# VectorE takes a tile's residual behind both softmax sums and the reciprocals, not between the sums

## What is computed

```python
x = x + cross_attention(layernorm(x), ctx)       # 16 heads of 32, 77 keys a batch
x = x + moe(layernorm(x))

# cross_attention: softmax(clip(q @ k.T * scale)) @ v, then @ Wo + bo
# moe: 8 experts, the 2 best logits of each token, softmax over the two,
#      at most 1024 tokens an expert (by rank), relu(tokens @ W1.T) @ W2.T,
#      times the gate, added back at the tokens' rows
```

## Time and profile before

| | us |
|---|---|
| median of 3 runs | 1440.36 |
| lowest, highest | 1437.39, 1440.61 |
| the profiled execution | 1436.3 |
| its span, first to last instruction | 1434.5 |

### The profile page before, as it was taken

One profiled execution on the slowest core, in us unless ns is written; L12 is line 12 of the kernel. 1 busy time (PEld: TensorE's weight loads), 2 busy tenths in 40 slices (PEclk: granted clock), 3 DMA queues, 4 the chain that ended last, 5 costly groups with the idle time before them and its releaser, 6 DMA issues.

```text
span 1434.5 us, 30528 instructions
## 1 busy us (share of the span) xinstructions
PE 1310.6 (91%) x12267; PEld 778.2 (54%) x12330; DVE 954.4 (67%) x1808; ACT 805.5 (56%) x1272; POOL 732.4 (51%) x781
## 2 busy tenths in 40 slices
PE   7649999989998999996849999999999999999996
PEld 3436777767676777674536444444444444444442
DVE  8668898889889887888775545454554545455421
ACT  4557888878998899987354515133341513334210
POOL 3187888877887778787323242242414123241301
PEclk9869999999999999998969999999999999999998
DMA  6147899978897786789433564655546455654401
GB/s 197 52 95 186 209 228 227 233 187 199 208 228 164 192 192 169 181 213 223 112 131 98 162 181 137 154 176 147 149 125 188 137 155 163 158 140 126 102 17 42
DMA packets 319574, 228.88 MB, mean 160 GB/s; under 512 B 253305, under 2 KB 253689, under 8 KB 319434
## 3 DMA queue, kind: packets, MB, share of 16 engines
q1 hardware_dynamic: 304074, 176.28, 50.0%
q0 software_dynamic: 15360, 50.66, 12.0%
HBM read 118.98 MB, written 50.86 MB: 118 GB/s over the span
## 4 chain that ended last, share of the span: by engine, by line
PE 74%; DVE 10%; POOL 7%; issue 4%; ACT 2%; SPq 2%; DMA 1%; DVEq 0%; POOLq 0%; ACTq 0%
PE ps L1208 23%; PE ps L1194 23%; PE ps L1094 9%; PE ps L1024 7%; PE ps L1075 3%; PE ps L1111 2%; PE ps L1008 2%; POOL sd L544 2%; DVE sm L1459 1%; PE ps L1047 1%; DVE x L1481 1%; PE ps L997 1%; POOL qT L524 1%; POOL ph L550 1%; POOL oT L530 1%
## 5 line engine op out<-in xcount | busy, mean ns | idle before, releaser
L1194 PE MATMUL ps<-xT,w1s 128*128 128x512 f16 (+1 forms) x1632 | 336.4, 368 | 1.9 <-DVE xT L1724 1.5
L1208 PE MATMUL ps<-w2s,hT 128*128 128x512 f16 x1536 | 332.8, 379 | 0.0
L846 ACT ACTIVATE hT<-ps 128x512 f16<-128x512 f32 (+1 forms) x136 | 77.8, 572 | 356.2 <-PE ps L1194 356.2
L1194 PEld LDWEIGHTS ps<-xT,w1s 128*128 128x128 f16 x1632 | 160.7, 99 | 175.4 <-issue 1.9
L1208 PEld LDWEIGHTS ps<-w2s,hT 128*128 128x128 f16 x1536 | 150.2, 98 | 181.3
L595 POOL DMA_INDIRECT out_dram<-ys,idx x64 | 71.7, 1120 | 278.4 <-DVE ys L1764 278.4
L1024 PE MATMUL ps<-xnT,wqh 128*128 128x256 f16 x1536 | 198.5, 282 | 3.8 <-ACT partq L734 3.7
L1094 PE MATMUL ps<-woh,oT 128*128 128x512 f16 x768 | 178.9, 381 | 9.4 <-POOL oT L530 3.6
L1754 DVE SCALAR_TENSOR_TENSOR hT<-ps,hT 128x512 f16<-128x512 f32 (+1 forms) x136 | 88.6, 658 | 138.4 <-ACT hT L846 138.3
L1764 DVE SCALAR_TENSOR_TENSOR ys<-ps,gs,og 128x512 f32<-128x512 f32 x64 | 48.0, 751 | 189.8 <-PE ps L1208 189.8
L550 POOL TENSOR_TENSOR ph<-sd,ph 128x1232 f16<-128x1232 f32 x64 | 162.3, 2535 | 18.8 <-ACT ph L757 18.1
(11 more groups left out here) (206 smaller groups left out, 1982.4 us busy)
## 6 DMA issues: line engine op xcount, KB each, us to landing
xr<-x SPq DMA_DIRECT2D x64, 256.0 KB, 3.5
xrow_dram<-x SPq DMA_DIRECT2D x64, 256.0 KB, 3.7
out_dram<-x SPq DMA_DIRECT2D x64, 256.0 KB, 4.0
stage<-w1T SPq DMA_DIRECT2D x8, 2048.0 KB, 9.5
stage<-w2T SPq DMA_DIRECT2D x8, 2048.0 KB, 8.4
xt<-x SPq DMA_DIRECT2D x59, 256.0 KB, 3.3
xs<-x SPq DMA_DIRECT2D x56, 256.0 KB, 4.2
wqf<-wq SPq DMA_DIRECT2D x1, 1024.0 KB, 7.3
```

The source lines that it names most:

```text
L1194: ins = pe.matmul(hb[z][:, 0:wide], w1s[e % 2][:, a, k, ic * P:(ic + 1) * P], xT[:, 4 * b + k, cols], start=(k == 0 and i == 0), stop=(k = ...
L1208: ins = pe.matmul(yb[z][:, :], hT[:, a, k, s * P:(s + 1) * P], w2s[e % 2][:, b, k, :], start=(k == 0 and i == 0), stop=(k == 7 and i == 2))
```

## The change

In the loop over beats -7 to 54 on VectorE, `residual(h)` moves from between the two sums to behind the reciprocals, and `add_slots` from ahead of the second sum to behind it. Nothing is added or removed, and no other engine's list changes. The loop over beats 55 to 63 has this order of sums, reciprocals and residual before and after.

```diff
@@ -1818,16 +1818,16 @@
                     route = ranking((h - 22) // 16)
                     steps(route, 1)
                 s_sum(h + 5, 0)
-                residual(h)
+                s_sum(h + 5, 1)
                 if H:
                     add_slots(H)
-                s_sum(h + 5, 1)
                 for g in ones_at(h):
                     value(g)
                 if H:
                     next_batch(H[-1])
                 steps(route, 4)
                 s_recip(h + 5)
+                residual(h)
                 tx_lo(h + 11)
                 ln2_stats(h)
                 ln2_aggr(h)
```

## The result

| | before | after |
|---|---|---|
| median of 6 runs, us | 1440.48 | 1455.05 |
| lowest, highest | 1437.39, 1445.77 | 1453.79, 1457.35 |
| the profiled execution (span) | 1436.3 (1434.5) | 1456.4 (1454.6) |
| ratio of times, 95% interval | | 1.010 (1.0086 to 1.0114) |

The changed kernel is 14.6 us slower. The forecast was 1464 with a range of 1446 to 1474: the direction and the mechanism held, the size was 9 us too large.

A forecast was written before the change was run, and what follows sets the result against it. TensorE was taken to set the pace, with hardly any idle time. Terms 0.8 - 3.6 + 5.6 + 4.4 + 3.1 + 3.6 + 13.2 = 27.1 us, 24 reaching the tail, made 1460.3, carried to the median 1464 (range 1446 to 1474).

The forecast's parts named there:

- the mechanism: Beats 0 to 54: value and steps ahead of the residual, some queueing behind GpSimd's L550, delay it and stall TensorE's L1075.
- L1075 waits for the residual: Sign to look for on TensorE: such waits in some 30 beats, together 35 to 45 us, in place of hardly any.
- the waits for L530: Sign to look for: TensorE's waits for GpSimd's low half of the attention output in beats 4 and 12 should be gone.
- odd beats without steps: Sign to look for: from one projection to the next, odd beats without routing keep their length.
- The sum: Beats 0 to 54: all gains and losses make TensorE 27.1 us late at beat 55; 24 us reach the tail.
- GpSimd's gain: Beats 4, 12, 28 and 44: the earlier reciprocal starts GpSimd sooner and removes TensorE's waits for L530, -3.6 us in all.
- Beats 2 and 10: Beats where VectorE itself is late: they lose 0.4 us each, +0.8.
- Value alone: Seven even beats without routing, 24 to 46: value queues behind L550 ahead of the residual, 0.6 to 0.9 us each, +5.6.
- The steps: Beats 16 to 23, 32 to 40, 48 to 54: routing steps delay the residual, +4.4, +3.1, +3.6, and +13.2 with value.
- L785: Beat 20: the first step of choice needs this ScalarE instruction, so L1075 starts at 318.27, not 316.80, 1.5 us lost.
- The tail: From beat 55: TensorE waits 4.58 us there for work following GpSimd, which is only some 24 us late; 24 us reach it.
- Rival (d): Waits over 2 us in beats 34, 50 and the tail lower the granted clock: up to 1474; chance 0.78 together with forecast.

The follow-up runs named there:

- e6: Changed kernel in its own order, with value reading its row of 64 numbers from PSUM in place of SBUF: 1446.63 us, ratio 1.0050.
- e7: e6 with ScalarE's exponential L785 moved ahead of two other ScalarE instructions in beats 20, 36 and 52: 1446.75 us, ratio 1.0053.
- e9: Changed kernel reordered so only the routing steps stand between both sums and the residual; slots, value and reciprocals follow it: 1456.21 us, ratio 1.0061.
- e4: Changed kernel with the residual right behind both sums, then slot addition, value, steps, and reciprocals last; first run 1433.48 us against 1439.07, ratio 0.9961.
- second run of e4's order: The kernel e4 again, unchanged, on another chip where the kernel before took 1448.80 us: 1448.13 us, ratio 1.0000.
- e1: Changed kernel with slot addition, value and next_batch moved behind the residual, steps and reciprocals staying ahead of it: 1453.08 us, ratio 1.0093.
- e10: Kernel before with only the routing steps moved, behind the reciprocals and L1425: 1457.08 us, ratio 1.0133.
- e8: Changed kernel with steps and reciprocals moved behind the residual, so only value and slots stand between sums and residual: 1455.02 us, ratio 1.0055.
- e4's third run: The kernel e4 a third time, unchanged, on a third chip: 1451.60 us against 1455.21 for the kernel before, ratio 0.9975.

## Why the prediction was right, and where its size was off

**What bounds it, and the mechanism: right.** TensorE sets the pace in both profiles. L1075 waits for the residual in 28 beats (some 30 foretold) for 35.8 us (35 to 45), starting 0.05 to 0.15 us behind its end; `value` takes 1.45 us in most even beats (1.3 foretold); the waits for L530 are gone; odd beats without steps keep their 9.21 us. e6, in which `value` doesn't queue, removes some 7 us. The prediction said that before's trace shows this queueing of `value` once, in beat 50; it also has a call of 1.38 us in the tail (689.08), under GpSimd's L530.

**The sum was 24 us at the end of the attention stage; the profiles show 17.1.** By groups, as the shift of the beats' first projection matmul between the two profiles, with what was foretold:

| | foretold | measured |
|---|---|---|
| beats 0 to 15 (with the gain of beats 4, 12) | -1.4 | -2.8 |
| 16 to 23 | 4.4 | 1.1 |
| 24 to 31 and 41 to 47 (with that of beats 28, 44) | 4.2 | 3.0 |
| 32 to 40 | 9.7 | 6.5 |
| 48 to 54 | 10.2 | 8.7 |
| sum | 27.1 | 16.5 |
| 55 to the end of the beats | -3 | 0.3 |

The measured shift stood at 0.3 us before beat 0, so it is 16.8 at beat 55 and 17.1 at beat 63.

*GpSimd's gain*: foretold 3.6, measured 1.25 in each of beats 4 and 12; if 28 and 44 lose the 0.67 of beats 30 and 46, it is 0.6 and 0.9 there, 4.0 in all. Beats 2 and 10, counted as losses of 0.4 each, gained 0.1 and 0.6; beat 13 lost 0.55. *Value alone*: a plain beat such as 30 or 46 loses 0.67, not 0.9; 24 loses 0.4; 26 and 42 lose -0.2 and 0 (their `value` doesn't queue and takes 0.41 us): 2.9 in all, where 5.6 was foretold. A wait of 1.6 us of L1024 for "issue", in beat 28, comes on top and belongs to no step of the change.

*The steps*: the term that was off most, 24.3 us foretold in beats 16 to 23, 32 to 40 and 48 to 54 and 16.2 measured. I worked each beat from its own rows of before, as though it began with before's lead. It doesn't: after TensorE has stood still for the residual, VectorE stands ahead in the next beat. Beat 51 shows it:

```profile
624.12 1.49 DVE L1459 TENSOR_REDUCE sm<-sd 128x8 f32<-128x616 f32 x2
625.65 0.19 DVE L1549 TENSOR_TENSOR dd<-dd,stt 128x16 f32<-128x16 f32 x1
...
626.40 0.24 DVE L1467 RECIPROCAL rr<-sm 128x16 f32<-128x16 f32 x1
627.26 0.75 DVE L1481 SCALAR_TENSOR_TENSOR x<-ps,scr,xr 128x512 f32<-128x512 f32 x1 [0.61 <-PE ps L1094]
```

Behind the 2.46 us for which TensorE waited in beat 50, the sums and all steps of beat 51 are over before its projection is, and L550 starts only at 626.05: L1549, which in before took 0.86 us in this beat, takes 0.19, and the residual even waits. I had foretold -0.1, 1.2 and 1.8 for beats 49 to 51; they lost -0.2, 2.45 and -0.1. Beat 35 is the same with a second effect: it gained 2.5 where 0.7 was to be lost, after beat 34 lost 2.3 in place of 0.9. Beat 22 gained 1.4 in place of 0.1: its step L1603 took 1.93 us under L550 in before, and misses it in after.

*L785*: I took beat 20's loss from it (1.5, measured 1.3), and in after VectorE does wait 3.0 us for it there. e7 shows that bringing it forward returns nothing, since L550 then holds the same step nearly as long. The size was right, but L785 was one of two waits that end together there, and I had named one.

*The tail*: I said that it would take up 3 us. It took up none (0.3 more). GpSimd's last L550 stand 15.9 to 16.6 us later than in before, TensorE 16.8: GpSimd had no lead over TensorE left to give. That it waits 39.4 us for ScalarE's L734, which itself follows TensorE's query product, fits this; no run tried it.

**Rival (d), the granted clock, was real but small.** Beat 34, TensorE, and the granted clock (the column behind POOL) of 3.9 us in that beat and of the 3.4 us behind the wait:

```profile
454.37 1.38 PE L1075 MATMUL ps<-pT,vb 128*32 128x256 f16 x36 [2.46 <-DVE x L1481]
455.68 0.97 PE L1047 MATMUL ps<-kb,qT 32*128 32x77 f16 x48
456.58 1.12 PE L1008 MATMUL ps<-identf,x 128*128 128x128 f32 x4
```

```profile
448.00:451.90 3.90, 3.90 (x30) 2.44 (x28) 3.74 (x9) 3.90 (x5) 2.96 (x4) 1.00 0.87 308
454.40:457.80 3.40, 3.40 (x90) 2.73 (x91) 3.06 (x6) 1.08 (x3) 2.99 (x7) 0.62 1.03 254
```

36 matmuls take 1.38 us (1.18 elsewhere), L1008's four 1.12 (0.66): part of it ran at 1.2 GHz, the lower of the two levels. Beats 34 and 50 each last 13.12 us, of which 9.1 is such a beat without its wait (beat 30: 9.85 - 0.74) and 2.46 the wait; the 1.5 us left are this. But the kernel before paid as well: in beat 35, after 3.8 us of waiting for L1425,

```profile
465.88 1.11 PE L1008 MATMUL ps<-identf,x 128*128 128x128 f32 x4 [3.82 <-DVE xnT L1425]
466.78 2.36 PE L1024 MATMUL ps<-xnT,wqh 128*128 128x256 f16 x12
```

against 1.47 for such an L1024. This wait is gone after the change, and with it the slow matmuls; I had given the waits of beats 19 and 35 back, but not the clock behind them. Beat 19 kept them, since L1075 now waits 4.05 us there. So two beats were slowed before (19, 35; by 1.7 and 1.4 us) and three after (19, 34, 50; by 1.6, 1.5 and 1.5, each time what is left of the beat without its wait, over 9.1 or 9.2 us): (d) leaves some 1.5 us. In beat 35 TensorE waits 2.57 us after the change, and no slow matmuls follow.

**Where the rest went.** The two profiled executions differ by 20.1 us, 17.1 of them by the end of the beats and 2.8 in the experts, where TensorE waited at L1194 for "issue" (see below). The medians differ by 14.6. So the change itself costs 14.6 to 17 us. What the runs separate: 10.0 us of the stretch come from value ahead of the residual (some 7 by its queueing, e6) and 14.7 from the steps there (e9). Against them stands what e4's order also gains, 3.6 us, and 2 us that the two share or that lie within the 3 us by which two profiles differ. The 2.8 us gained before beat 16 were not tried separately, nor was the slot addition.

## What to carry to other kernels

Before an instruction is moved, ask under which instruction of the other engine it will now run: a VectorE operation with two SBUF inputs of 0.41 us became one of 1.45 or 2.2 us by its place alone, and giving it one input in PSUM restored it. Where VectorE releases a long GpSimd operation, issue the release last, behind everything that would queue under it; here that was worth 20 to 25 us between two orders that differ in nothing else. Moving up what a held instruction waits for brings nothing if the next thing that holds it ends no sooner (e7). And when stalls are added up beat by beat, carry the lead forward: a stall of the bounding engine gives the others time in the next beat, and the sum of single beats comes out too large (27.1 us here, 16.5 measured).

## What the runs showed of the hardware that was not expected

A tensor_scalar on 16 columns (L1565) queued for 2.09 us under L544, though it has a single tensor input. The Trainium skill, page "SBUF — State Buffer", section "Who interferes with whom", names tensor_scalar among the operations that can take both ports, and by that the trace agrees; which mode this one ran in no trace shows. The sums (tensor_reduce, at most 0.79 us) and L1655 (one input in PSUM, at most 0.23 us) kept their length in every profile.

TensorE in the expert stage waited, in some executions and on some chips, for nothing that the profile names. The matmuls' waits in the second run of e4's order, then in the changed kernel:

```profile
PE ps L1194 <- issue: 9.9, 15, 1.3
```

```profile
PE ps L1194 <- issue: 1.4, 4, 0.6
```

In the profile of the kernel before and in those of e1 to e7 (e4's first run) and e10 no matmul of L1194 waits so; e8 and e9, on the chip of e4's second run, have 6.0 and 7.5 us, and e4's third run has 12.3. The expert stage (from the first to the last matmul of L1208) takes 621.4 us in the profiles without them, 624.2 in the changed kernel's, 631.6 and 632.1 in e8's and e9's, 636.2 and 641.9 in those of the second and third run of e4's order, on chips where the kernel before took 1448.8 and 1455.2 us. One order has them on two chips and not on a third, so they don't come with VectorE's order, and they hide a gain of 4 us in a measurement of the whole. What causes them stays open.
